# Edge attention on one core: normalisation on VectorE alone, and the linear term turned by transposes

## The reference, cut to what matters

```python
h = jnp.maximum(_layernorm(x, axis=-1), 0.0)
Xq, Xv = (h @ W_lin.T), (h @ W_val.T)               # each cut into 4 heads of 64
e = einsum('behd,hd->beh', leaky_relu(Xq[:, src] + Xq[:, dst], 0.2), a)
e = e + log(A0[src, dst] + 1e-8)
attn = exp(e - segment_max(e, src)); attn = attn / segment_sum(attn, src)
Y = segment_sum(attn * Xv[:, dst], src)
x = x + Y @ W_out.T
```

## Time and profile before

| | |
|---|---|
| Median of 3 runs | 2062.48 us |
| The profiled execution: time | 2061.53 us |
| The profiled execution: span from first to last instruction | 2060.0 us |
| TensorE busy | 1970.3 us (96%) |
| VectorE, ScalarE, GpSimd busy | 1248.8, 989.9, 224.6 us |
| Mean granted clock of TensorE | 0.981 of full speed |
| Attention layer, about | 1134 to 1655 us |

### The profile page before, as it was taken

The page is one execution under the profiler, slowest core; times in us unless marked ns, Lnnn a source line. Parts: engine busy times, 40 slices in busy tenths (PEclk is TensorE's granted clock), DMA queues, the critical chain, the costliest instruction groups (busy, mean ns, idle before and its releaser), DMA issues. The chain is left out here.

```text
span 2060.0 us, 32417 instructions
## 1 busy us (share of the span) xinstructions
PE 1970.3 (96%) x11982; PEld 1600.4 (78%) x11982; DVE 1248.8 (61%) x2549; ACT 989.9 (48%) x1619; POOL 224.6 (11%) x194
## 2 busy tenths in 40 slices
PE   7999999999999999999999899999999899897998
PEld 6998888888888889888887556657566688686998
DVE  7454665454445455554753766665664588897786
ACT  2554664333333333433332464563636246575996
POOL 1000000000111111011011450110100011100000
PEclk8999999999999999999999999999999999998999
DMA  3101001000100000100002321423314032001232
GB/s 118 55 29 41 0 0 41 0 0 0 41 1 1 0 0 1 32 1 41 41 0 82 133 72 52 145 83 95 102 38 148 26 102 69 22 0 51 83 103 92
DMA packets 81491, 99.99 MB, mean 49 GB/s; under 512 B 7408, under 2 KB 73584, under 8 KB 79088
## 3 DMA queue, kind: packets, MB, share of 16 engines
q1 hardware_dynamic: 81392, 98.65, 14.5%
HBM read 61.78 MB, written 33.55 MB: 46 GB/s over the span
## 5 line engine op out<-in xcount | busy, mean ns | idle before, releaser
L706 ACT ACTIVATE b_gate<-b_pG,b_bias 128x512 f32<-128x512 f32 (+2 forms) x460 | 295.0, 669 | 367.9 <-PE b_pG L55 367.0
L53 PE MATMUL b_pG<-b_xshi,b_whi 128*128 128x512 f32 (+2 forms) x920 | 351.5, 382 | 2.2 <-PEq L299 1.4
L55 PE MATMUL b_pG<-b_xshi,b_wlo 128*128 128x512 f32 (+2 forms) x920 | 351.3, 382 | 0.0
L54 PE MATMUL b_pG<-b_xslo,b_whi 128*128 128x512 f32 (+2 forms) x920 | 351.2, 382 | 0.0
L756 DVE CAST b_xshi<-HT 128x512 fp32r<-128x512 f32 (+3 forms) x130 | 57.3, 483 | 284.8 <-PE b_pG L55 268.3
L53 PEld LDWEIGHTS b_pG<-b_xshi,b_whi 128*128 128x128 f32 x920 | 172.7, 188 | 35.4 <-issue 3.1
L54 PEld LDWEIGHTS b_pG<-b_xslo,b_whi 128*128 128x128 f32 x920 | 172.7, 188 | 32.5
L55 PEld LDWEIGHTS b_pG<-b_xshi,b_wlo 128*128 128x128 f32 x920 | 172.7, 188 | 32.4
L55 PE MATMUL b_pG<-b_hshi,b_wlo 128*128 128x512 f32 (+2 forms) x512 | 194.3, 380 | 0.0
L54 PE MATMUL b_pG<-b_hslo,b_whi 128*128 128x512 f32 (+2 forms) x512 | 194.3, 380 | 0.0
L53 PE MATMUL b_pG<-b_hshi,b_whi 128*128 128x512 f32 (+2 forms) x512 | 194.3, 379 | 0.0
(11 more groups left out here) (366 smaller groups left out, 3986.2 us busy)
## 6 DMA issues: line engine op xcount, KB each, us to landing
a_xt<-in_x SPq DMA_DIRECT2D x16, 512.0 KB, 5.8
h_scratch<-HT SPq DMA_DIRECT2D x4, 2048.0 KB, 6.9
l_x<-in_x SPq DMA_DIRECT2D x16, 512.0 KB, 3.4
l_w<-h_scratch SPq DMA_DIRECT2D x16, 512.0 KB, 5.2
x_scratch<-l_x SPq DMA_DIRECT2D x16, 512.0 KB, 3.3
c_x<-x_scratch SPq DMA_DIRECT2D x32, 256.0 KB, 3.6
x_scratch<-c_x SPq DMA_DIRECT2D x32, 256.0 KB, 2.6
l_x<-x_scratch SPq DMA_DIRECT2D x16, 512.0 KB, 3.8
```

Source lines behind the costliest of these rows:

```text
L53: nc.tensor.matmul(out, w_hi, x_hi, start=first, stop=False)
L54: nc.tensor.matmul(out, w_hi, x_lo, start=False, stop=False)
L55: return nc.tensor.matmul(out, w_lo, x_hi, start=False, stop=last)
L706: nc.scalar.activation(gate[s][:, g, 0:plan.n], pG[s][:, g, 0:plan.n], SIG[g], bias=bias[:, plan.p - 1, 2 * g + s:2 * g + s + 1])\
```

## The change

VectorE normalises all four tiles of a group, and GpSimd only makes the root. The semaphore `normed` therefore counts one step for a group in place of two. The pair products are split three, three and two, behind groups 2, 3 and 4, and each batch now waits until VectorE has normalised that group. The linear term is turned by four plain transposes of 128x128, so that the strips stand side by side in the PSUM bank, and VectorE adds the four strips: four reductions of 64 partitions each in place of two copies. The table `strip` goes.

```diff
-    NT = 2
@@ GpSimd
-                def normalise(q, m):
+                def root(q, m):
                     G = NJ * q + m
                     pool.wait_ge(sem["var_eps"], G + 1)
+                    wait(pool, sem["normed"], G)
                     nc.gpsimd.tensor_tensor(rstd[:, :], ve[:, :], mhalf[:, :], ALU.pow).then_inc(sem["rstd_ready"], 1)
-                    pool.wait_ge(sem["rstd_ready"], 2 * G + 1)
-                    xn = hst[m % 2][:, :, :].rearrange("p k (a d) -> p (k a) d", d=D)
-                    shape = [P, GT - NT, D]
-                    nc.gpsimd.tensor_tensor(xn[:, NT:, :], xt[m % 2][:, NT:, :],
-                                            mv[:, NT:, 0:1].to_broadcast(shape), ALU.subtract).then_inc(sem["rstd_ready"], 1)
-                    pool.wait_ge(sem["rstd_ready"], 2 * G + 2)
-                    nc.gpsimd.tensor_tensor(xn[:, NT:, :], xn[:, NT:, :], rstd[:, NT:].unsqueeze(2).to_broadcast(shape),
-                                            ALU.mult).then_inc(sem["normed"], 1)
...
-                        normalise(q, m)
-                        if isinstance(q, int) and q == 0 and m == 3:
-                            make_pairs(3, NP)
+                        root(q, m)
+                        if isinstance(q, int) and q == 0 and m in (3, 4):
+                            pool.wait_ge(sem["normed"], m + 1)
+                            make_pairs(3 * (m - 2), min(3 * (m - 1), NP))
...
                 pool.wait_ge(tables.made, ONE_HOT)
+                pool.wait_ge(sem["normed"], 3)
                 make_pairs(0, 3)
@@ TensorE
-                    pe.wait_ge(sem["normed"], 2 * (NJ * q + m + 1))
+                    pe.wait_ge(sem["normed"], NJ * q + m + 1)
...
-                        last = nc.tensor.matmul(lin_bank(m, 1)[:, HEADS * t:HEADS * (t + 1)], lin_row[:, t * P:(t + 1) * P], tab["strip"][:, :],
-                                                start=True, stop=True)
+                        c = slice(t * P, (t + 1) * P)
+                        last = nc.tensor.transpose(lin_bank(m, 1)[:, c], lin_row[:, c], tab["ident"][:, :])
@@ VectorE
-                    for t in range(NT):
+                    for t in range(GT):
                         last = V.tensor_scalar(xn[:, t, :], xt[m % 2][:, t, :], mv[:, t, 0:1],
                                                rstd[:, t:t + 1], ALU.subtract, ALU.mult)
...
-                    part = lin_bank(m, 1)[:, 0:GT * HEADS].rearrange("p (t k h) -> p k t h", t=GT, k=KD)
+                    part = lin_bank(m, 1).rearrange("p (t s c) -> p c t s", t=GT, c=SLOTS)
                     rows = lin_cols(lin, m // NJ)
                     tiles = slice(GT * (m % NJ), GT * (m % NJ) + GT)
-                    for i, r in enumerate(halves):
-                        last = V.tensor_copy(rows[r, i, :, tiles, :], part[r])
+                    for k in range(KD):
+                        for i, r in enumerate(halves):
+                            last = V.tensor_reduce(rows[r, i, k, tiles, :].rearrange("p t h -> p h t"), part[r, 2 * k:2 * k + 2], AX.X, ALU.add)
```

More of the change, by code:

```diff
@@ L165, in __init__ @@
                 ("wo_hi", [P, KD, D], F32R), ("wo_lo", [P, KD, D], F32R), ("wl", [P, KD, SLOTS], F32),
-                ("strip", [P, HEADS], F32), ("sign", [P, KD, 2 * SLOTS - 2], F32), ("cut", [P, EDGES + 1], F32)]
+                ("sign", [P, KD, 2 * SLOTS - 2], F32), ("cut", [P, EDGES + 1], F32)]
         self.tab, place = {}, {}
@@ L793, in spread_ends @@
                     V.memset(tab["wl"][:, :, :], 0.0)
-                    V.tensor_reduce(tab["strip"][:, :], tab["ident"][:, :].rearrange("p (s c) -> p c s", c=SLOTS)[:, 0:HEADS, :],
-                                    AX.X, ALU.add)
                     link(V.memset(tab["sign"][:, :, :], 0.0))
@@ L1115, in body @@
                     for m in range(3, NJ if last else NJ + 3):
-                        normalise(q, m)
-                        if isinstance(q, int) and q == 0 and m == 3:
-                            make_pairs(3, NP)
-                normalise(0, 0)
-                normalise(0, 1)
-                normalise(0, 2)
+                        root(q, m)
+                        if isinstance(q, int) and q == 0 and m in (3, 4):
+                            pool.wait_ge(sem["normed"], m + 1)
+                            make_pairs(3 * (m - 2), min(3 * (m - 1), NP))
+                root(0, 0)
+                root(0, 1)
+                root(0, 2)
                 pool.wait_ge(spilled[0], 16)
@@ L1483, in measure @@
                     dve.wait_ge(sem["x1_done"], G + 1)
-                    wait(dve, sem["rstd_ready"], 2 * G)
+                    wait(dve, sem["rstd_ready"], G)
                     V.memset(ve[:, :], EPS)
@@ L1492, in moments @@
                     dve.wait_ge(sem["stats"], 2 * G + 1)
-                    wait(dve, sem["normed"], 2 * G)
+                    wait(dve, sem["normed"], G)
                     V.memset(unused[:, :], 0.0)
@@ L1502, in normalise @@
                     G = NJ * q + m
-                    dve.wait_ge(sem["rstd_ready"], 2 * G + 1)
+                    dve.wait_ge(sem["rstd_ready"], G + 1)
                     xn = hst[m % 2][:, :, :].rearrange("p k (a d) -> p (k a) d", d=D)
-                    for t in range(NT):
+                    for t in range(GT):
                         last = V.tensor_scalar(xn[:, t, :], xt[m % 2][:, t, :], mv[:, t, 0:1],
```

## The result

The changed kernel takes 2039.28 us (median of 4 runs, 2038.4 to 2045.12), the kernel before 2062.14 us (median of 4, with one more run beside the three of before): a ratio of 0.9894, 95% interval 0.9878 to 0.9910. In a second comparison it took 2038.15 us against 2061.58: 0.9894 again. The forecast was 2042.5 us. The profiled execution took 2038.40 us, its span is 2036.5 us.

What follows compares the result with a forecast made beforehand. The prediction took TensorE to bound the kernel, busy 96% of the span. Its terms, 11.7 + 4.9 + 3.2 - 0.8 = 19.0 us, taken from 2061.53 gave 2042.5 us (75% for this sum), range 2035 to 2051.

Steps and rivals of the forecast that it cites:

- Part 1: Steady groups: VectorE normalises all four tiles in 1.37 us instead of 2.35; 0.9 us a group, 11.7 us over thirteen.
- modelled idle time (0.55): Floor of the normalisation's gain per group: TensorE's waits of 0.32 us at the turn and 0.23 at the projection.
- the hand-over (0.98): Upper end of the normalisation's gain per group: the turn hands over sooner, so the projection starts 0.98 us earlier.
- Part 2: Steady groups: four transposes replace the linear term's small matmuls on TensorE; 0.38 us a group, 4.9 us over thirteen.
- The slack: Steady group: reductions end 0.66 us before TensorE's turn-back needs them, costing nothing unless each takes over 0.36 us.
- Part 3: Groups 3 to 5: with pair products split and held back, the variance add is no longer stuck; 3.2 us gained.
- Part 4: Start of the layer: VectorE is late there, so the added reductions delay the turn-back; a cost of 0.8 us.
- the turn-back forecast near 1183.8: Start of the layer: TensorE's turn-back, at 1182.96 before, was to come 0.8 us later.
- A: Rival, 14%: only the first wait is recovered and a new one replaces the second; half of 0.9 us left, 2048.4 us.
- B: Rival, 4% with costs like it: strided reductions take 0.69 us each, the linear term comes 1.31 us late; 2059.5 us.
- C: Rival, 4%: VectorE's 1.13 us per normalisation comes from its own operands, not GpSimd; four cost 4.5 us, 2083.5 us total.
- D: Rival, 3%: TensorE's clock falls once in each group because of the transposes, 0.79 us each, 11 us; 2053.5 us.

Runs made afterwards that it cites:

- the products beside the normalisations: The changed kernel with GpSimd doing two products on a spare 128x512 tile behind each root, beside VectorE's four normalisations; 2063.16 us (one run).
- the pair products not held back: The changed kernel with the pair products in their old places, three and five, and no wait for `normed`; 2062.14 us, ratio 1.0001.
- the doubled set: The changed kernel with the four reductions done a second time into a spare tile, before the real ones; 2054.79 us (one run).
- the cuts later: The changed kernel with the two instructions that build the cut table moved from the first group to behind group 5's root; 2035.61 us, ratio 0.9872.
- strips alone: The changed kernel with the linear term of the layer's first two groups turned by strip-table matmuls and two copies, as before; 2037.68 us, ratio 0.9887.

## Why the prediction was right

**Part 1, the normalisation (0.9 us in a group forecast, 1.00 measured).** The four take 1.38 us, forecast 1.37. The step from modelled idle time (0.55) to the hand-over (0.98) was the one that counted, and the upper end was right: the projection starts 2.76 us after the first normalisation, 0.97 less. The 0.08 us left for ScalarE wasn't needed. That the neighbour's products were the cause is shown by two experiments, the products beside the normalisations and the pair products not held back. The Trainium skill ("SBUF — State Buffer", on who interferes with whom) says that a tensor_scalar can enter a mode in which it contends with GpSimd, that a tensor_tensor with both inputs in SBUF contends with GpSimd's reads, and that an instruction with at most one SBUF input outside such a mode does not. The trace agrees: beside the pair products normalisations and cuts take 2.7 to 3.7 us, and the copy of values out of PSUM at 1176.98 takes its 0.42. Not every instruction from SBUF to SBUF waits either: in the kernel before, VectorE's statistics of the rows, with one input, kept the 1.06 us for three that they take elsewhere, in the middle of the five pair products (1193.48 to 1211.49):

```profile
1206.12 1.06 DVE L1487 BATCH_NORM_STATS2 c_st<-l_x 128x6 f32<-128x256 f32 x3
```

**Part 2, the linear term (0.38 forecast, 0.45 measured).** The four transposes hold TensorE 0.36 us (forecast 0.43), and a reduction took the 189 ns of the forecast. The slack was put at 0.66 us, with a threshold of 0.36 us for a reduction; the doubled set shows 0.31 to 0.42 us, a threshold of about 0.28 to 0.30. The sum didn't hang on it.

**Part 3, the pair products (3.2 forecast, 3.2 measured, 3.3 alone).** Right, with one thing missing: the wait for `normed` was treated as part of the same term, but it protects part 1. With neither it nor the split the change is worth nothing (1.0001).

**Part 4, the start of the layer (0.8 forecast, 3.15 measured at group 3's root).** This is the term that was mis-sized, and it had nothing in it for the clock; the turn-back forecast near 1183.8 stands at 1185.75. Its working holds at one clock: +0.88 for two sets of reductions, -0.25 from group 2's root to group 3's (22.39 against 22.64, the faster normalisation less a third set, both with one fall of the clock), and 0.23 before group 1's root (-0.23 in its second profiled execution). The missing 2.29 us is a fall of TensorE to 1.2 GHz between groups 1 and 2, which the kernel before did not have in its profiled execution. The wait ahead of it is no longer than before, by the timeline of before and of after:

```profile
1147.17 1.12 PE L1355 MATMUL c_pZ<-c_relu,s_ones 64*128 64x512 f32 x2 [1.98 <-DVE c_relu L1705]
```

```profile
1146.94 2.07 PE L1347 MATMUL c_pZ<-c_relu,s_ones 64*128 64x512 f32 x2 [1.98 <-DVE c_relu L1698]
```

The same matmul after the same 1.98 us of idle time, at 2.4 GHz in one and at 1.2 in the other. The fall is there in all eleven profiled executions that have one or both halves of the change (in five by this matmul, in six only behind it), and not in the two without (before, and the split of the products alone). What decides it was not found. It cost 1.6 us where the stretch stands at 0.93, 2.3 in the changed kernel's first execution (0.86) and 3.4 with the cuts later (0.81).

**The sum.** 19.0 us was forecast and the layer gave 19.7: 2.5 us more by the thirteen groups (19.1 against 16.6), 0.6 more in the rest of the layer, where the kernel before lost 1.5 us to its clock, and 2.3 less at the start. That the two agree so closely is luck: the forecast had no term for the clock in either place, and it took from the gain at the start and added to it in the output phase. The other 3.3 us of the measured span lie behind the layer, as said above. The prediction put them at nothing ("nothing in the later layers changes, they only start earlier"), and they are as large as the distance from its 2042.5 us to the 2039.28 measured.

**The rivals.** A: ScalarE's relu does become the next to be waited for, but by VectorE (1.34 us), not by TensorE. B: reductions took 0.20 us, not 0.69. C: refuted by the 407 ns. D: the steady group ran at 1.00 with twenty transposes in it; the rule of the Trainium skill ("TensorE: Matmul & The Clock Gate", Part 4) that transposes don't count as busy shows no effect there.

## What to carry to other kernels

Work on GpSimd that reads and writes SBUF can be charged to VectorE as well: here each normalisation, each of the two table instructions and the 128x4 addition that met a product waited until one had ended, while the statistics and the instructions that read PSUM did not. So look in the trace for which of VectorE's instructions are stretched, take short shared work off GpSimd, and put its long instructions where VectorE runs the others. If an edit speeds up one engine's step, look at what its neighbour's next instruction now falls on; here holding back and splitting the long products was worth the whole gain. Compare short stretches of two traces only at the same granted clock.

## What the runs showed of the hardware

- VectorE beside GpSimd: a 128x256 normalisation took 0.35 us alone, about 1.13 beside a product of 1.04 us and 3.64 beside products of 3.62. Two table instructions of 128x511 and 128x513 took 0.69 and 0.43 us alone, 2.69 and 3.73 beside products. Three statistics of 128x256 took 1.06 us in both places.
- Idle time alone doesn't decide a fall of TensorE's clock. With strips alone the turn-back waits 3.18 us and the stretch stays at 1.00; in the changed kernel it waits 3.17 and the stretch is at 0.92. One fall cost 1.4 us at the least and 3.4 at the most (25.89 - 21.63 - 0.88, in the run with the cuts later).
- Four fp32 transposes of 128x128 (0.36 us) hold TensorE for less than half the time of four fp32 matmuls with 4 columns (0.81 us), which the trace shows as eight instructions.
